# Other places for the running-maximum items of a step in a one-core cross-attention kernel

## The chip, the cores and the metric

The kernel runs on one core of a Trainium2 chip. The metric is the device time of one execution in microseconds (us), median over runs; lower is better. TensorE (PE in the profile) multiplies, VectorE (DVE), ScalarE (ACT) and GpSimd (POOL) work on its results, and SyncE (SP) issues most transfers.

## The reference, cut to what matters

```python
x = layernorm(hidden_states) * ln_gamma + ln_beta        # hidden_states: 2 x 512 x 1024
Q = split_heads(x @ Wq.T)                                # 32 heads of 32
K = split_heads(memory_keys); V = split_heads(memory_keys)   # the context: 2 x 1024 x 1024
scores = einsum('bhsd,bhtd->bhst', Q, K) * 32 ** -0.5    # masked
probs = softmax(scores)
attn = einsum('bhst,bhtd->bhsd', probs, V)
out = residual + merge_heads(attn) @ Wout.T
```

## The kernel before, in words

Sixteen steps (0 to 15) carry the attention; a step is one group of four heads of one batch. Before them the queries are projected, after them the output is projected. A step has eight tiles of 128 context positions. For a tile, TensorE makes four score blocks of 128x512 (one for each head, `score`, L947), in three PSUM banks SX used in turn; ScalarE makes each one's exponential (L615); then the probabilities are multiplied with the values (`values`, L963, eight small matmuls into 32 columns each), one tile later.

Beside this stream runs a second one through two larger PSUM buffers MX, used in turn. Its items belong to other steps and are woven between scores and values:

- `max`: the maximum over keys for a later step. Two score matmuls of 97x512 (`max_item`, L923), then one 128x1024 reduce on VectorE (L737). There are 16 of them for each step, numbered 0 to 15.
- `keys`: eight transposes of the keys of the step two ahead (`keys_item`, L863); ScalarE copies their rounded high part (L541, KTh), VectorE makes the rest (L700, KTl), and only then is the buffer free. SyncE then sends both, and the split queries (L730, L732), to the stacked rows R.
- `bias`: the transposed maxima (L928), copied by ScalarE (L569) and VectorE (L743) and sent to R for the next step's scores.
- `sums`: the row sums of the previous step's probabilities (L953, 24 matmuls); VectorE transposes them (L753).
- `wout`: transposed output weights, in the last two steps alone.

Three lists say where items stand. In a tile, TensorE's order is: scores of heads 0 and 1; the slot's first part (`early`); the previous tile's values; the second part (`with_01`); scores of heads 2 and 3; the third part (`with_23`):

```python
score(n, u, tt, 0); score(n, u, tt, 1)
for item in early: mx_item(*item)
values(n, u, tt - 1)
for item in with_01: mx_item(*item)
score(n, u, tt, 2); score(n, u, tt, 3)
for item in with_23: mx_item(*item)
```

The values of tile 0 are those of the last tile of the step before. Each item waits first, in TensorE's own queue, for the buffer that it takes:

```python
pe.wait_ge(mx_freed, freed - (kind != "bias" or last_kind != ("max", M_ITEMS - 1)))
```

`freed` counts all items before this one, so an item other than the bias goes when all but its immediate predecessor have been released, and the bias when all have. `mx_freed` is raised by VectorE alone, in the order of the items: by the reduce of a `max`, after KTl for `keys`, after BTl for `bias`, after the transpose for `sums`. VectorE walks through the same lists; after a tile's items it adds the reciprocal (tile 2) and the second transpose (tile 3) of the row sums. GpSimd adds up probability tiles 0 to 5 (L486) and normalises (L474).

`FIRST_STEP` places the items of step 0, `STEP` those of steps 1 to 14 (`maxima(a, i)` is item i for the step a ahead). Items for steps past the last are dropped: step 14 has no `keys(2)` and no `maxima(2, ...)`, and step 15 has lists of its own. Steps 1 to 12 are a loop with four steps in its body; 13 to 15 are written out.

Of the kernel before, what the change touches and what calls it, by code (L numbers as in the profile page):

```python
# [66 lines left out]
def keys(a):  # L67
    return [("keys", a, 0)]


def maxima(a, *items):
    return [("max", a, i) for i in items]
# [6 lines left out]
def bias(a):  # L79
    return [("bias", a, 0)]  # L80
# [6 lines left out]
def sums(a):  # L87
    return [("sums", a, 0)]
# [14 lines left out]
    ([], bias(1) + maxima(2, 0), maxima(2, 1, 2, 3)),  # L103
]
STEP = [
    ([], maxima(1, 4), keys(2)),
    ([], sums(-1), maxima(1, 5)),
    ([], maxima(1, 6), maxima(1, 7)),
    (maxima(1, 8), maxima(1, 9), maxima(1, 10)),
    ([], maxima(1, 11), maxima(1, 12)),  # L110
    (maxima(1, 13), maxima(1, 14), maxima(1, 15)),
    ([], bias(1) + maxima(2, 0), maxima(2, 1)),
    ([], maxima(2, 2), maxima(2, 3)),
]


# [1005 lines left out]
```

## Time and profile before

| | |
|---|---|
| median of three runs | 724.67 us (724.27 to 725.08) |
| the profiled execution, its own time | 724.74 us |
| its span, first to last instruction | 722.9 us |
| mean granted TensorE clock | 0.983 |
| TensorE busy with matmuls | 679.7 us, 94% of the span |
| VectorE / ScalarE / GpSimd busy | 460.7 / 339.4 / 392.1 us |
| attention steps 1 to 14 | about 187 to 599 us |

Times in rows are microseconds from the span's start. A row of the timeline is a run of like instructions: start, length, engine, line, output and input, count, and in brackets the idle time ahead of it with what ended it. Matmul ends are modelled, so that neighbouring rows overlap; distances between starts are the safer measure. PEld is the load of weights.

### The profile page before, as it was taken

Reading aid. Unit: us, or ns where it says so; the run is one execution under the profiler, and the core shown is the slowest. Engines: PE = TensorE matmul, PEld = TensorE weight load, DVE = VectorE, ACT = ScalarE, POOL = GpSimd, SP = SyncE. Lnnn points to the kernel's source line nnn. Section 1 sums busy time; section 2 is a strip of 40 time slices with the busy share of each in tenths; the row PEclk is TensorE's granted clock in tenths of the full one; section 3 lists DMA queues with packets and bytes.
Section 4 is the critical chain, followed back from the end, with each engine's and each line's share of the span. In section 5 each row is a group of like instructions: output and inputs, shape, how many; then the busy total and the mean of one; then the engine's idle time right before and its main releaser. Section 6 shows DMA issues by size and latency. Waiting matters only on the chain.

```text
span 722.9 us, 10760 instructions
## 1 busy us (share of the span) xinstructions
PE 679.7 (94%) x3537; PEld 396.9 (55%) x3537; DVE 460.7 (64%) x494; ACT 339.4 (47%) x614; POOL 392.1 (54%) x107
## 2 busy tenths in 40 slices
PE   2789999777999999999999999999999999899998
PEld 2568787633444444444445445454445445478886
DVE  6763333058787787877877868778687676643231
ACT  3741211252566656566666565665666566500000
POOL 1000000054397887967979769797797797910000
PEclk9999999976999999999999999999999999999999
DMA  9611000533335154261442523525325103123231
GB/s 339 189 51 53 30 29 1 135 69 98 75 89 141 51 131 101 64 156 43 123 118 61 143 60 103 133 57 131 85 76 132 60 2 118 58 92 116 84 116 58
DMA packets 40286, 68.10 MB, mean 94 GB/s; under 512 B 5668, under 2 KB 22694, under 8 KB 40238
## 3 DMA queue, kind: packets, MB, share of 16 engines
q1 hardware_dynamic: 39700, 66.85, 33.8%
q10 hardware_dynamic: 548, 0.80, 0.4%
q8 instruction: 17, 0.28, 0.2%
q14 instruction: 21, 0.17, 0.1%
HBM read 25.18 MB, written 4.19 MB: 41 GB/s over the span
## 4 chain that ended last, share of the span: by engine, by line
PE 87%; DVE 5%; ACT 3%; SPq 2%; DMA 2%; issue 2%; POOL 0%; ACTq 0%; DVEq 0%; POOLq 0%
PE MX L923 20%; PE PV L963 18%; PE SX L947 18%; PE MX L1081 12%; PE MX L953 5%; PE SX L886 5%; PE PV L886 4%; PE MX L863 2%; ACT PR L615 1%; PE SX L878 1%; PE MX L933 1%; DMA PR<-in_x 1%; ACT PR L525 1%; PE MX L857 1%; DVE QT L732 1%
## 5 line engine op out<-in xcount | busy, mean ns | idle before, releaser
L737 DVE TENSOR_REDUCE mx<-MX 128x1 f32<-128x1024 f32 x256 | 302.1, 1217 | 107.9 <-PE MX L923 103.3
L615 ACT ACTIVATE PR<-SX 128x512 f32<-128x512 f32 x512 | 269.0, 600 | 173.9 <-PE SX L947 168.4
L486 POOL TENSOR_TENSOR acc<-acc,PR 128x2048 f32<-128x2048 f32 x64 | 293.5, 4587 | 18.0 <-ACT PR L615 11.8
L486 POOL TENSOR_TENSOR acc<-PR 128x2048 f32<-128x2048 f32 x16 | 73.5, 4592 | 224.2 <-ACT PR L615 224.2
L923 PE MATMUL MX<-R 97*128 97x512 f32 x512 | 175.9, 427 | 11.3 <-DVE mx L737 9.2
L947 PE MATMUL SX<-R 99*128 99x512 f32 x512 | 175.4, 420 | 7.5 <-DMA R<-BTl 4.1
L923 PEld LDWEIGHTS MX<-R 97*128 97x128 f32 x512 | 85.6, 190 | 107.9 <-DVE mx L737 89.7
L963 PE MATMUL PV<-PR,C 128*32 128x512 f32 x1024 | 139.0, 615 | 0.1
L947 PEld LDWEIGHTS SX<-R 99*128 99x128 f32 x512 | 94.5, 191 | 70.7 <-ACT PR L615 35.4
L832 DVE TENSOR_TENSOR PR<-PR,MX 128x512 f32<-128x512 f32 x16 | 10.9, 687 | 53.3 <-PE MX L1081 51.9
L1081 PE MATMUL MX<-R 128*128 128x512 f32 x192 | 44.3, 390 | 0.0
L963 PEld LDWEIGHTS PV<-PR,C 128*32 128x32 f32 x1024 | 20.3, 108 | 41.7 <-ACT PR L615 36.8
L1081 PEld LDWEIGHTS MX<-R 128*128 128x128 f32 x192 | 36.0, 188 | 8.3 <-issue 0.8
L1081 PE MATMUL MX<-R,KTh 128*128 128x512 f32 x128 | 40.2, 390 | 0.0
L886 PE MATMUL PV<-R 128*128 128x512 f32 x120 | 31.3, 408 | 0.2 <-DVE R L696 0.2
L700 DVE TENSOR_TENSOR KTl<-MX,KTh 128x1024 fp32r<-128x1024 f32 x15 | 18.4, 1225 | 19.2 <-ACT KTh L541 19.2
L953 PE MATMUL MX<-PR,ones 128*32 128x512 f32 x240 | 28.5, 592 | 0.0
L1081 PEld LDWEIGHTS MX<-R,KTh 128*128 128x128 f32 x128 | 24.0, 188 | 5.8 <-issue 0.8
L474 POOL TENSOR_TENSOR QA<-QA,rsum 128x512 f32 (+1 forms) x16 | 20.7, 1293 | 11.5 <-DVE rsum L759 11.5
L563 ACT ACTIVATE QA<-SX 128x512 f32<-128x512 f32 x8 | 4.8, 598 | 46.7 <-PE SX L886 39.4
L886 PE MATMUL SX<-R,KTh 128*128 128x512 f32 x80 | 25.5, 389 | 0.0
L1081 PE MATMUL MX<-R,KTl 128*128 128x512 f32 x64 | 24.9, 389 | 0.0
(84 smaller groups left out, 478.5 us busy)
## 6 DMA issues: line engine op xcount, KB each, us to landing
R<-KTh SPq DMA_DIRECT2D x60, 256.0 KB, 4.3
PR<-in_x SPq DMA_DIRECT2D x16, 512.0 KB, 4.1
C<-in_ctx SPq DMA_DIRECT2D x16, 512.0 KB, 3.5
R<-KTl SPq DMA_DIRECT2D x60, 128.0 KB, 3.9
R<-QT SPq DMA_DIRECT2D x60, 128.0 KB, 2.5
acc<-in_L_xattn_Wq SPq DMA_DIRECT2D x8, 512.0 KB, 3.5
C<-in_L_xattn_Wout SPq DMA_DIRECT2D x8, 512.0 KB, 3.3
R<-QT SPq DMA_DIRECT2D x60, 64.0 KB, 2.1
```

The lines of the kernel that those rows point to most:

```text
L474: nc.gpsimd.tensor_tensor(at, at, rsum[:, :], ALU.mult).then_inc(attn_done, 1)
L486: nc.gpsimd.tensor_tensor(acc[:, :, :], a, PR[:, tt % RING, :, :], ALU.add).then_inc(pool_used, 1)
L615: nc.scalar.activation(PR[:, tt % RING, h, :], SX[(HPG * tt + h) % BANKS][:, :], ACT.Exp, scale=SCALE).then_inc(exp_done, 1)
L700: nc.vector.tensor_tensor(KTl[:, :], MX[par][:, :], KTh[:, :].bitcast(F32), ALU.subtract).then_inc(kt_lo, 1)
L737: nc.vector.tensor_reduce(mx[:, u % 2, i:i + 1], MX[par][:, :], mybir.AxisListType.X, ALU.max, negate=True).then_inc(mx_freed, 1)
L863: ins = nc.tensor.transpose(MX[par][:, t * P:(t + 1) * P], C[u % RING][:, t, :], ident[:, :])
L886: ins = nc.tensor.matmul(QP[b if bank is None else bank][:, :], w[W_IN[g]][:, k * P:(k + 1) * P], v[b][:, k, :], start=(k == 0 and o == 0) ...
L923: ins = nc.tensor.matmul(MX[par][:, cs], QS[u % RING][0:BIAS, h, st * P:(st + 1) * P], KS[u % RING][0:BIAS, h, cs], start=True, stop=True)
L947: nc.tensor.matmul(SX[at % BANKS][:, :], KS[u % RING][0:ROWS, h, tt * P:(tt + 1) * P], QS[u % RING][0:ROWS, h, :], start=True, stop=True). ...
L953: ins = nc.tensor.matmul(bank[h * HD:(h + 1) * HD, :], ones[:, :], tile(h), start=start, stop=stop, skip_group_check=True)
L963: ins = nc.tensor.matmul(PV[h * HD:(h + 1) * HD, :], C[u % RING][:, tt, h * HD:(h + 1) * HD], PR[:, tt % RING, h, :], start=(tt == 0), sto ...
L1081: ins = nc.tensor.matmul(MX[1 - q][:, cs], a[q][:, g, :], w[half][:, g, :], start=(g == 0 and o == 0), stop=(g == GROUPS - 1 and o == 2))
```

## The change

The 16 maxima of a step keep their order, as do keys, bias and sums between their neighbours in VectorE's list, except that the keys come one maximum later and the sums two. A tile's first item now stands ahead of its values, in `early`, and not behind them. Tiles 0 and 1 have three items instead of two; tiles 3 and 5 have two instead of three. `FIRST_STEP` is as before.

```diff
 STEP = [
-    ([], maxima(1, 4), keys(2)),
-    ([], sums(-1), maxima(1, 5)),
-    ([], maxima(1, 6), maxima(1, 7)),
-    (maxima(1, 8), maxima(1, 9), maxima(1, 10)),
-    ([], maxima(1, 11), maxima(1, 12)),
-    (maxima(1, 13), maxima(1, 14), maxima(1, 15)),
+    (maxima(1, 4), maxima(1, 5), keys(2)),
+    (maxima(1, 6), sums(-1), maxima(1, 7)),
+    (maxima(1, 8), [], maxima(1, 9)),
+    (maxima(1, 10), [], maxima(1, 11)),
+    (maxima(1, 12), [], maxima(1, 13)),
+    (maxima(1, 14), [], maxima(1, 15)),
     ([], bias(1) + maxima(2, 0), maxima(2, 1)),
-    ([], maxima(2, 2), maxima(2, 3)),
+    (maxima(2, 2), [], maxima(2, 3)),
 ]
```

## Rows read from the trace of the kernel before

**Rows 1.** The page: engines' busy time, share of the span, instructions.

```profile
PE 679.7 (94%) x3537; PEld 396.9 (55%) x3537; DVE 460.7 (64%) x494; ACT 339.4 (47%) x614; POOL 392.1 (54%) x107
```

**Rows 2.** The page: the chain that ended last, by engine.

```profile
PE 87%; DVE 5%; ACT 3%; SPq 2%; DMA 2%; issue 2%; POOL 0%; ACTq 0%; DVEq 0%; POOLq 0%
```

**Rows 3.** Timeline of TensorE, tiles 3 and 4 of step 5.

```profile
317.27 0.65 PE L947 MATMUL SX<-R 99*128 99x512 f32 x2
317.81 0.73 PE L923 MATMUL MX<-R 97*128 97x512 f32 x2
318.47 1.06 PE L963 MATMUL PV<-PR,C 128*32 128x512 f32 x8
319.47 0.73 PE L923 MATMUL MX<-R 97*128 97x512 f32 x2
...
320.51 0.63 PE L923 MATMUL MX<-R 97*128 97x512 f32 x2
320.98 0.65 PE L947 MATMUL SX<-R 99*128 99x512 f32 x2
321.61 1.06 PE L963 MATMUL PV<-PR,C 128*32 128x512 f32 x8
...
324.12 0.65 PE L947 MATMUL SX<-R 99*128 99x512 f32 x2
```

**Rows 4.** Timeline: weight loads of two maxima, and VectorE's reduces beside them.

```profile
316.57 0.42 PEld L923 LDWEIGHTS MX<-R 97*128 97x128 f32 x2
...
317.81 0.30 PEld L923 LDWEIGHTS MX<-R 97*128 97x128 f32 x2 [0.20 <-DVE mx L737]
```

**Rows 5.** Timeline of VectorE: the reduces of maxima 6 and 7 in step 5.

```profile
316.53 2.36 DVE L737 TENSOR_REDUCE mx<-MX 128x1 f32<-128x1024 f32 x2 [0.98 <-PE MX L923]
```

**Rows 6.** Timeline: tiles 6 and 7 of step 5, VectorE and TensorE.

```profile
330.75 2.35 DVE L737 TENSOR_REDUCE mx<-MX 128x1 f32<-128x1024 f32 x2 [0.23 <-DVE BTl L743]
...
331.20 0.63 PE L947 MATMUL SX<-R 99*128 99x512 f32 x2
```

**Rows 7.** Timeline: tiles 0 and 1 of step 6, all engines.

```profile
334.45 0.99 PE L947 MATMUL SX<-R 99*128 99x512 f32 x2
...
337.14 1.23 DVE L737 TENSOR_REDUCE mx<-MX 128x1 f32<-128x1024 f32 x1 [1.22 <-PE MX L923]
...
337.41 1.04 PE L863 MATMUL MX<-ident,C 128*128 128x128 f32 x8
...
338.56 1.03 ACT L541 ACTIVATE KTh<-MX 128x1024 fp32r<-128x1024 f32 x1
...
339.62 1.23 DVE L700 TENSOR_TENSOR KTl<-MX,KTh 128x1024 fp32r<-128x1024 f32 x1 [1.26 <-ACT KTh L541]
...
339.73 1.90 PE L953 MATMUL MX<-PR,ones 128*32 128x512 f32 x16
```

**Rows 8.** Timeline: tiles 0 and 1 of step 5, the first of a loop body.

```profile
307.56 0.51 PE L947 MATMUL SX<-R 99*128 99x512 f32 x1 [0.44 <-ACT PR L615]
...
307.90 1.04 PE L863 MATMUL MX<-ident,C 128*128 128x128 f32 x8
...
310.40 1.90 PE L953 MATMUL MX<-PR,ones 128*32 128x512 f32 x16
310.41 1.23 DVE L700 TENSOR_TENSOR KTl<-MX,KTh 128x1024 fp32r<-128x1024 f32 x1 [2.27 <-ACT KTh L541]
```

**Rows 9.** Timeline: the same place in step 9.

```profile
425.45 0.51 PE L947 MATMUL SX<-R 99*128 99x512 f32 x1 [0.16 <-ACT PR L615]
```

**Rows 10.** Timeline: the end of step 0 and the start of step 1.

```profile
184.29 4.62 DVE L737 TENSOR_REDUCE mx<-MX 128x1 f32<-128x1024 f32 x4
...
187.26 0.62 PE L947 MATMUL SX<-R 99*128 99x512 f32 x2
```

**Rows 11.** Timeline of SyncE's queue: last issue of query rows, and bias, in step 6.

```profile
353.08 0.59 SPq L329 DMA_DIRECT2D R<-QT  x1
359.87 0.52 SPq L350 DMA_DIRECT2D R<-BTh  x1
```

## The prediction, made before the changed kernel was run

> **What bounds the kernel now.** I read first the engines' busy time [rows 1]: TensorE is busy for 94% of the span, and no other engine for more than 64%. The chain that ended last says the same [rows 2]: 87% of it is TensorE's own work. So in the attention steps the end is set by the number of TensorE instructions and by the moments in which TensorE's queue waits. The edit adds no work and takes none away. It can only remove waits and make new ones, and the timeline of one step shows where.
>
> The distance from a pair of scores to the next pair is the cost of a tile. Tile 4, with two maxima, runs from 320.98 to 324.12: 3.14 us. Tile 3, with three, runs from 317.27 to 320.98: 3.71 us [rows 3]. A maximum in an ordinary place costs 0.47 us (320.51 to 320.98); the early third one costs 3.71 - 3.14 = 0.57. Why 0.10 more: maximum 8 needs the buffer of maximum 6, whose reduce starts at 316.53. I take 1.23 us for a reduce [rows 5, 7], so it ends at 317.76, and the weights of maximum 8 are loaded at 317.81 with VectorE named as the releaser [rows 4]. From a reduce's end to the load pass 0.05 us.
>
> **The change, part by part.**
>
> Tiles 2 to 5. Before they cost 2 x 3.14 + 2 x 3.71 = 13.70 us and hold ten maxima. Now they hold eight. A new tile is scores, early maximum, values, scores, maximum. The pieces, by the distance to the next start [rows 3]: scores 0.47 or 0.48 (as at 320.51 for a maximum), the maximum ahead of values 0.63 (317.81 to 318.47 is 0.66 with its load exposed, 320.98 to 321.61 is 0.63 for scores ahead of values), values 1.00 (318.47 to 319.47), then a pair behind values and one more 1.04 (319.47 to 320.51): 3.15 us. The same pieces stand in a tile without an early item, only in another order. Is the early maximum free to go? It needs the reduce of the early one a tile back, over two microseconds ahead; VectorE spends 2.4 us on two reduces [rows 5] of a 3.15 us tile, and tiles 2 and 3 add a reciprocal and a transpose, together under a microsecond. I followed VectorE's queue through these tiles and find at most 0.05 us of wait, at maximum 14. So tiles 2 to 5 cost 4 x 3.15 = 12.60, 1.10 less. Two maxima at 0.47 (0.94) have gone to tiles 0 and 1, so the true gain is 0.16 a step. It is the two waits of 0.10 us less the 0.04 that four tiles of 3.15 cost over 3.14.
>
> Tiles 0 and 1, the first new wait. Before, the order was maximum 4, keys | sums, maximum 5. The sums needed only the buffer of maximum 4. Now it is 4, 5, keys | 6, sums, 7: the sums take the buffer of maximum 5, but have to wait for everything but their immediate predecessor 6, and so for the keys' release. That release is slow: transposes on TensorE from 337.41, ScalarE's copy at 338.56, VectorE's subtraction 339.62 to 340.85 [rows 7]. From the keys' start it is 3.44, with the signal 3.49 us. TensorE's cover from the keys' start to the sums is 339.73 - 337.41 = 2.32 us, plus now maximum 6: 2.79. The sums wait for 3.49 - 2.79 = 0.70 us, and behind them in TensorE's queue wait everything: scores, and so ScalarE's exponentials. ScalarE can't start the copy sooner, since it starts 0.1 us after the transposes end; nor can VectorE, which is idle for 1.26 us ahead of its part [rows 7]. Next late would be maximum 6's reduce, behind the subtraction and the query split; it ends near the end of the 2.6 us of sums, before maximum 7 wants it. SyncE's key and query rows start 0.47 us later. The last is issued at 353.08, the maxima that read them start in tile 6, beside the bias whose rows are sent at 359.87 [rows 11], so nothing waits.
>
> The order ahead of the keys is free: maximum 4's reduce, 337.14 to 338.37 before, stays about where it was less a microsecond since its matmuls move ahead of the values, and maximum 5's takes its place and ends near 338.85, when maximum 6 wants to be loaded.
>
> Tile 7, the second new wait. Maximum 2 now stands right behind the first scores, at 331.20 + 0.47 = 331.67. It needs the reduce of maximum 0, which starts only at 330.75 since VectorE makes the bias first [rows 6], and ends at 331.98. The load is then at 332.03, the values 0.66 behind at 332.69, where without a wait they would be at 331.67 + 0.63 = 332.30. It costs 0.39 us. Before, the values stood in between and covered it. The stall at the start of the next step (0.99 us for a pair of scores at 334.45 [rows 7]) does not absorb this: it comes from exponentials that are themselves released by the scores two places back, and so moves along.
>
> Whether a waiting maximum's load could be hidden decides a small part. In an ordinary place the load starts ahead of the matmul (316.57), in a waiting one with it (317.81 for both) [rows 3, 4]; so I charge it. The Trainium skill, TensorE: Matmul & The Clock Gate, section "Architectural detail: the array is 16× 32×32, not 1× 128×128", says that TensorE's queue can pull weight loads ahead of matmuls in flight. By that rule the tile 7 term would be 0.36 and the sum some 0.4 us lower; the trace shows it for loads that wait for nothing.
>
> Steps. Keys and both new waits exist in steps 1 to 13: 13 x (0.70 + 0.39 - 0.16) = 12.1 us. Three corrections. At steps 5 and 9, the starts of a loop body, ScalarE comes late and TensorE already waits for it, at 307.56 and 425.45 [rows 8, 9]. The added maximum fills that wait: the keys stay at 307.90, the release is at 310.41 + 1.23 + 0.05 = 311.69, the sums slip from 310.40 by 1.29, of which 0.94 is the two maxima. That is 0.35 in place of 0.70: -0.7 for both. In step 1 maximum 4 needs the reduce of maximum 2, third of four that start at 184.29 (ending near 187.8) [rows 10], and is loaded about 0.1 to 0.2 late: +0.2. Step 14 has the tiles 2 to 5 alone: -0.16. Sum: 12.1 - 0.7 + 0.2 - 0.2 = 11.4 us.
>
> Bounds. The wait of the sums could be as low as 0.5 (a release that comes a little sooner since ScalarE is less pressed) and as high as 0.9 (a restart of the 32-column matmuls, for which no row stands); the tile 7 wait 0.25 to 0.5; the gain of tiles 2 to 5 up to 0.3, or down to nothing if VectorE's backlog reaches maximum 14. Over 13 steps the ends are about 0.45 and 1.4 a step, some 5 and 18 us; not all at once, so for the range I hold 6 to 15.
>
> **The rivals.**
>
> 1. Forecast: both waits appear. 724.7 + 11.4 = 736.1 us. The profiled execution (724.74) is within 0.1 of the median, so the sum stands against either.
> 2. Only the sums' wait: the tile 7 wait is covered, if maximum 0's reduce came 0.4 us sooner or the matmuls ahead ran later. For it: only 0.39 us and a chain of three engines. Against it: the times at 330.75 and 331.67 leave no cover. 11.4 - 13 x 0.39 = 6.3: 731.0.
> 3. Only the tile 7 wait: the keys' chain gets shorter by 0.7 us. Against it: ScalarE and VectorE already start within 0.1 us. Eleven steps at 0.70 and two at 0.35 are 8.4; 11.4 - 8.4 = 3.0: 727.7.
> 4. The other side, faster: the item buffers are never what TensorE waits for, and only the two released reduces and the filled stalls at loop starts count. The mechanism is that the keys' release reaches TensorE within its cover; it decides from 0.70 us sooner on, and the same must hold in tile 7. 13 x -0.16, another -0.9 for the maxima that fill the stalls at steps 5 and 9 (0.47 each at most), -0.2 for step 14: -3.2, so 721.5. For it: ScalarE and VectorE have free time at both places. Against it: the free time lies behind TensorE's own output, not ahead of it.
> 5. Backlog: VectorE, pushed back 1.6 us at tile 1 by both the split queries and maximum 6, doesn't catch up before maximum 14 and the bias, which waits for maximum 15's reduce; another 0.3 us a step, 740.
> 6. Nothing changes, if each wait removed is one made: within 0.2%, 724.7. It needs the new waits to be a sixth of what I find.
>
> From a maximum to the values pass 0.66 us where to scores it is 0.47 [rows 3]; the change of matmul shape costs that. The values are still entered and left once a tile, and values and sums stay neighbours in tile 1, so the sum has nothing for it.
>
> **How the numbers follow.** Chances: forecast 0.66, only the sums' wait 0.11, only tile 7 0.06, faster 0.05, no change 0.03, backlog 0.09. The predicted time is the forecast's, 736.1. The range from 730.5 to 740.0 takes in rivals 2 and 5 and leaves out 3, 4 and 6 and a little of the forecast's tails, under 2 in 10. A measurement of this kernel can tell about 0.2% (1.4 us) from no change. Faster by more than that 0.05, within it 0.04 (rival 6 and a part of 3), slower 0.91.
>
> **What the profile after would show.** In an ordinary step: a gap of 0.6 to 0.8 us ahead of the first matmuls of L953, released by VectorE's KTl (L700) or its release; in tile 7 a load of L923 weights some 0.05 us behind the end of the first reduce after BTl; tiles 2 to 5 of 3.15 us each with loads of early maxima ahead of their matmuls; the step 30.2 us where it is 29.3. At steps 5 and 9 no wait of L947 over 0.3 us for the exponential, and a slip of about 1.3 for the sums. The prediction is wrong if the sums start without a gap (then the release is not what I take it for), if the values in tile 7 are not held, or if waits of over 0.1 us stand at maxima 10, 12 or 14 (then VectorE's backlog is larger than I worked out).

## The result and the profile after

The changed kernel takes 732.28 us (median of four runs, 731.71 to 733.42) where the kernel before takes 724.47 beside it: a ratio of 1.0109, 95% interval 1.0093 to 1.0125, slower by about 8 us. The prediction said 736.1 with a range of 730.5 to 740.0. The direction and both waits that it named are there; its sum was 11.4 us and the measured difference is 7.8. The profiled execution took 731.71 us with a span of 729.9.

The page of the changed kernel, engines and the chain that ended last:

```profile
PE 677.1 (93%) x3537; PEld 390.7 (54%) x3537; DVE 462.8 (63%) x494; ACT 340.8 (47%) x614; POOL 392.6 (54%) x107
...
PE 75%; DVE 9%; ACT 6%; POOL 3%; issue 3%; SPq 2%; DMA 2%; ACTq 0%; DVEq 0%; POOLq 0%
```

The work is the same as in [rows 1]. The chain [rows 2] was 87% TensorE; now it leaves TensorE for VectorE and ScalarE in every step. The granted clock is 1.00 from 200 to 600 us in both kernels, so the steps don't differ by the clock. The view of waits, from 200 to 610 us, says where (engine, line, releaser: us in total, times, longest):

```profile
PEld SX L947 <- ACT PR L615: 72.1, 155, 0.8
...
PEld MX L953 <- DVEq L702: 18.3, 12, 1.7
...
PEld MX L923 <- DVE mx L737: 8.0, 13, 0.6
...
PE MX L953 <- DVEq L702: 7.4, 12, 0.8
```

The first line looks the largest and costs little: 49 of its 72.1 us are stretches of 0.84 us in which no weights are loaded while the values run, put down to ScalarE. L702 is the release of the keys' buffer: twelve steps in this window, twelve waits. The thirteen of L923 answer to maximum 2 in tile 7.

Since the stream is in order, a step is best read by where its blocks of values start. These are the L963 rows of step 6 in the changed kernel, tiles 0 to 7, and the first of step 7:

```profile
339.94 1.06 PE L963 MATMUL PV<-PR,C 128*32 128x512 f32 x8
...
343.85 1.06 PE L963 MATMUL PV<-PR,C 128*32 128x512 f32 x8
...
350.30 1.06 PE L963 MATMUL PV<-PR,C 128*32 128x512 f32 x8
...
353.37 1.06 PE L963 MATMUL PV<-PR,C 128*32 128x512 f32 x8
...
356.43 1.07 PE L963 MATMUL PV<-PR,C 128*32 128x512 f32 x8
...
359.50 1.06 PE L963 MATMUL PV<-PR,C 128*32 128x512 f32 x8
...
362.17 1.06 PE L963 MATMUL PV<-PR,C 128*32 128x512 f32 x8
...
366.36 1.07 PE L963 MATMUL PV<-PR,C 128*32 128x512 f32 x8
...
369.93 1.06 PE L963 MATMUL PV<-PR,C 128*32 128x512 f32 x8
```

Their distances, as medians over steps 1 to 12 of each trace (worked out from such rows; d0 is from the block in tile 0 to that in tile 1, d7 leads into the next step), for both kernels and the versions tried below, with the medians of the timed runs:

```
                       d0    d1    d2    d3    d4    d5    d6    d7   step   time us
before                3.48  5.25  3.70  3.14  3.71  3.14  3.34  3.57  29.33  724.47
after                 3.91  6.46  3.08  3.08  3.07  2.67  4.19  3.56  30.03  732.28
x1 tile 7 back        3.94  6.44  3.08  3.07  3.08  2.67  3.26  4.03  29.57  727.57
x2 sums not waiting   3.49  5.65  3.71  3.07  3.08  2.67  4.19  3.57  29.43  724.22
x3 both               3.48  5.65  3.71  3.07  3.08  2.67  3.26  4.03  28.95  718.14
x4 two tiles alone    3.47  5.65  3.08  3.70  3.07  3.13  3.35  3.57  29.02  719.84
x7 tile 7 part alone  3.47  5.24  3.71  3.14  3.72  3.14  4.24  3.10  29.74  729.07
x8 none ahead         3.95  6.03  3.13  3.14  3.13  3.14  3.35  4.03  29.90  731.46
x9 bias behind        3.47  5.65  3.70  3.08  3.08  3.11  3.14  3.57  28.79  717.01
```

Before against after: 0.7 us a step, with gains in d2 to d5 that are partly items moved elsewhere, and losses in d0 (0.43, all of it one maximum), d1 (1.21, of which one maximum is about 0.40) and d6 (0.85, of which one maximum is 0.47). From the block in tile 0 of step 1 to that of step 15 the trace grows from 411.45 to 418.46 us. Ahead of that stretch stands the maximum added to step 1, with 0.66. Together this is 7.7 of the 7.8 us.

**The wait of the sums.** TensorE, ScalarE and VectorE in step 6 of the changed kernel:

```profile
341.96 1.04 PE L863 MATMUL MX<-ident,C 128*128 128x128 f32 x8
...
343.12 1.03 ACT L541 ACTIVATE KTh<-MX 128x1024 fp32r<-128x1024 f32 x1
...
344.18 1.23 DVE L700 TENSOR_TENSOR KTl<-MX,KTh 128x1024 fp32r<-128x1024 f32 x1 [1.26 <-ACT KTh L541]
345.51 0.16 PEld L953 LDWEIGHTS MX<-PR,ones 128*32 128x32 f32 x8 [1.51 <-DVEq L702]
345.51 1.92 PE L953 MATMUL MX<-PR,ones 128*32 128x512 f32 x16 [0.60 <-DVEq L702]
```

From the keys' start to the subtraction's end are 3.45 us, as in [rows 7]. The sums start 0.10 us after that and 3.55 after the keys, where they used to start 2.32 after them. Behind the values they would have started at 343.85 + 0.88 = 344.73 (0.88 is their distance in the trace of before); they start 0.78 later.

**The wait of maximum 2** in tile 7, same step:

```profile
364.42 3.49 DVE L737 TENSOR_REDUCE mx<-MX 128x1 f32<-128x1024 f32 x3 [0.23 <-DVE BTl L743]
364.88 0.63 PE L947 MATMUL SX<-R 99*128 99x512 f32 x2
365.70 0.30 PEld L923 LDWEIGHTS MX<-R 97*128 97x128 f32 x2 [0.63 <-DVE mx L737]
365.70 0.73 PE L923 MATMUL MX<-R 97*128 97x512 f32 x2 [0.19 <-DVE mx L737]
```

The reduce of maximum 0 starts at 364.42 and takes 1.23; the load follows at 365.70, where the matmul was due at 364.88 + 0.47 = 365.35. It is the picture that the prediction drew from [rows 6].

**What it did not draw**, tile 3 of the changed kernel:

```profile
355.40 0.64 PE L947 MATMUL SX<-R 99*128 99x512 f32 x2
355.55 0.19 PEld L947 LDWEIGHTS SX<-R 99*128 99x128 f32 x1 [0.18 <-ACT PR L615]
...
355.65 0.42 PEld L923 LDWEIGHTS MX<-R 97*128 97x128 f32 x2
355.88 0.62 PE L923 MATMUL MX<-R 97*128 97x512 f32 x2
```

The second score of the pair waits for ScalarE (0.18), as it did before, but the maximum follows at the ordinary 0.48 and the values start 0.55 behind the maximum (356.43), not 0.63. The new tile takes 3.07 us and not the 3.15 of the prediction.

### The profile page after: what moved, and what is told of

Its sections match the earlier page's. It is cut to its first block, busy times and chain, and to the rows that moved or that the text cites. A ratio compares the mean times of both kernels' runs of the same rounds, so it can differ in the third digit from the quotient of the medians.

```text
span 729.9 us, 10760 instructions
## 1 busy us (share of the span) xinstructions
PE 677.1 (93%) x3537; PEld 390.7 (54%) x3537; DVE 462.8 (63%) x494; ACT 340.8 (47%) x614; POOL 392.6 (54%) x107
## 3 DMA queue, kind: packets, MB, share of 16 engines
HBM read 25.18 MB, written 4.19 MB: 40 GB/s over the span
## 4 chain that ended last, share of the span: by engine, by line
PE 75%; DVE 9%; ACT 6%; POOL 3%; issue 3%; SPq 2%; DMA 2%; ACTq 0%; DVEq 0%; POOLq 0%
PE SX L947 16%; PE PV L963 15%; PE MX L923 14%; PE MX L1081 12%; PE MX L953 6%; PE PV L886 5%; PE SX L886 4%; POOL acc L486 3%; DVE mx L737 3%; DVE KTl L700 2%; ACT KTh L541 2%; ACT PR L615 2%; PE SX L878 1%; DMA PR<-in_x 1%; PE MX L933 1%
## 5 line engine op out<-in xcount | busy, mean ns | idle before, releaser
L737 DVE TENSOR_REDUCE mx<-MX 128x1 f32<-128x1024 f32 x256 | 305.3, 1215 | 112.8 <-PE MX L923 108.1
L947 PE MATMUL SX<-R 99*128 99x512 f32 x512 | 181.1, 432 | 6.7 <-DMA R<-BTl 3.9
L923 PE MATMUL MX<-R 97*128 97x512 f32 x512 | 167.7, 411 | 13.6 <-DVE mx L737 11.4
L947 PEld LDWEIGHTS SX<-R 99*128 99x128 f32 x512 | 88.5, 190 | 119.1 <-ACT PR L615 82.4
L963 PE MATMUL PV<-PR,C 128*32 128x512 f32 x1024 | 138.0, 611 | 0.1
L923 PEld LDWEIGHTS MX<-R 97*128 97x128 f32 x512 | 93.0, 192 | 57.2 <-DVE mx L737 24.0
L963 PEld LDWEIGHTS PV<-PR,C 128*32 128x32 f32 x1024 | 20.2, 108 | 45.3 <-issue 31.3
L953 PE MATMUL MX<-PR,ones 128*32 128x512 f32 x240 | 28.8, 597 | 8.0 <-DVEq L702 8.0
L886 PEld LDWEIGHTS PV<-R 128*128 128x128 f32 x120 | 22.8, 199 | 4.8 <-DVE R L696 0.7
```

The source lines that it names most:

```text
L737: nc.vector.tensor_reduce(mx[:, u % 2, i:i + 1], MX[par][:, :], mybir.AxisListType.X, ALU.max, negate=True).then_inc(mx_freed, 1)
L886: ins = nc.tensor.matmul(QP[b if bank is None else bank][:, :], w[W_IN[g]][:, k * P:(k + 1) * P], v[b][:, k, :], start=(k == 0 and o == 0) ...
L923: ins = nc.tensor.matmul(MX[par][:, cs], QS[u % RING][0:BIAS, h, st * P:(st + 1) * P], KS[u % RING][0:BIAS, h, cs], start=True, stop=True)
L947: nc.tensor.matmul(SX[at % BANKS][:, :], KS[u % RING][0:ROWS, h, tt * P:(tt + 1) * P], QS[u % RING][0:ROWS, h, :], start=True, stop=True). ...
L953: ins = nc.tensor.matmul(bank[h * HD:(h + 1) * HD, :], ones[:, :], tile(h), start=start, stop=stop, skip_group_check=True)
L963: ins = nc.tensor.matmul(PV[h * HD:(h + 1) * HD, :], C[u % RING][:, tt, h * HD:(h + 1) * HD], PR[:, tt % RING, h, :], start=(tt == 0), sto ...
```

## The experiments

The first four ask whether the two waits are what costs, whether they add, and what the places ahead of the values are worth. Each is timed in five rounds beside the kernel before.

**x1: tile 7 as before.**

```diff
-    (maxima(2, 2), [], maxima(2, 3)),
+    ([], maxima(2, 2), maxima(2, 3)),
```

> The changed kernel with one edit: in tile 7 maximum 2 stands behind the values again. Theory (two new waits): its wait for the reduce of maximum 0, about 0.37 us in each of 13 steps, goes, and 0.08 comes back since the values again follow directly on a score that waited for ScalarE. 13 x -0.29 = -3.8: near 728.5 us, tile 6 to 7 from 4.19 to about 3.4 us and tile 7 about 0.5 longer. Rival (the order of these items is of no account, the time sits with VectorE or ScalarE and only moves on to maximum 3 or to the next step): no change, 732.3.

Measured: 727.57 us, 1.0048 of the kernel before (1.0028 to 1.0069), 4.7 less than the changed kernel (across two sets of runs). The step falls by 0.46 where 0.29 was expected. d6 + d7 fall from 7.75 to 7.29, by the whole of the wait, and the 0.08 does not come back: d6 without its maximum is 3.26, less than the 3.34 of before. Part of this belongs to the bias, which experiment x8 separates.

**x2: the sums with the keys as immediate predecessor.** The sums now take the other buffer, and tile 2 has three items.

```diff
-    (maxima(1, 6), sums(-1), maxima(1, 7)),
-    (maxima(1, 8), [], maxima(1, 9)),
+    ([], sums(-1), maxima(1, 6)),
+    (maxima(1, 7), maxima(1, 8), maxima(1, 9)),
```

> The changed kernel with tile 1 as (nothing; sums; maximum 6) and tile 2 as (7, 8, 9): now the keys are the immediate predecessor of the sums, which so don't wait for their release. Theory: the wait of about 0.78 us at L953 goes in each of 13 steps, 0.08 comes back in tile 1; 13 x -0.70 = -9.1: near 723.2 us, less at steps 5 and 9. Rival (VectorE's backlog, since the reduces of 6 to 10 now come close behind the transpose of the sums): waits of 0.3 us or more at maxima 8 and 10 take half of it, 728 us or more.

Measured: 724.22 us, 1.0007 (0.9993 to 1.0022). Its step 6:

```profile
337.37 1.04 PE L863 MATMUL MX<-ident,C 128*128 128x128 f32 x8
...
339.58 1.23 DVE L700 TENSOR_TENSOR KTl<-MX,KTh 128x1024 fp32r<-128x1024 f32 x1 [1.26 <-ACT KTh L541]
339.70 1.90 PE L953 MATMUL MX<-PR,ones 128*32 128x512 f32 x16
```

The keys' chain is as slow as ever, but the sums start 2.33 us after the keys and no longer wait for its end. d1 falls from 6.46 to 5.65, 0.81: that is what the wait costs. The step falls by 0.60, not 0.70: d0 + d1 lose the wait and one maximum (0.42), d2 gains one and pays 0.63 for it. Three maxima between two blocks of values cost 0.57 to 0.63 for the third in every timed version that has them (3.70 or 3.71 against 3.07 or 3.14), since the third comes too soon for the reduce two back. Here that is maximum 10, whose load waits 0.20 us for the reduce of maximum 8 (at 347.51); the rival wanted waits of 0.3 us or more at maxima 8 and 10, and they did not appear.

**x3: both edits.**

> Both edits together: sums without the keys ahead by two, and maximum 2 behind the values in tile 7. If the two waits are separate things their gains add: -3.8 and -9.1, near 719.4 us, under the kernel before by 5 us. Rival: the two share VectorE's or ScalarE's time and the gains don't add; then it is no faster than the better one alone, 723.

Measured: 718.14 us, 0.9916 (0.9898 to 0.9933). The step is 28.95: 1.08 below the changed kernel, and the two singly gave 0.46 and 0.60. The waits are separate and add. This version is faster than the kernel before by 6 us.

**x4: the kernel before with a maximum ahead of the values in tiles 2 and 4 alone.**

```diff
-    ([], maxima(1, 6), maxima(1, 7)),
+    (maxima(1, 6), [], maxima(1, 7)),
...
-    ([], maxima(1, 11), maxima(1, 12)),
+    (maxima(1, 11), [], maxima(1, 12)),
```

> The kernel before with one part of the change alone: in tiles 2 and 4 the first maximum stands ahead of the values, all else as before. Theory that the second score's wait for ScalarE (0.08 us) is covered by a maximum between it and the values, and that the third items in tiles 3 and 5 lose their wait because the reduces start earlier: tiles 2 and 4 at 3.06 us where they were 3.14, tiles 3 and 5 at 3.53 to 3.55 where they were 3.71; -0.5 in 14 steps, near 717.5 us. Rival, the prediction's own reckoning, in which only the 0.10 us waits at maxima 8 and 13 go: -0.2 a step, near 721.7. Second rival: nothing, 724.5.

Measured: 719.84 us, 0.9939 (0.9923 to 0.9955): 4.3 us, between the two expectations (7 and 2.8). The step falls by 0.31. The two distances that now hold two maxima with one ahead of the values, d2 and d4, are 3.08 and 3.07, as expected. What was wrong is the hope for the third items. This load of maximum 11 in step 6 shows the wait in its new place:

```profile
350.00 0.30 PEld L923 LDWEIGHTS MX<-R 97*128 97x128 f32 x2 [0.21 <-DVE mx L737]
```

Of two such waits (maxima 8 and 13 before) one is left, at 11, because the ten maxima after the sums are spread otherwise: d1 takes one more, at 0.40.

The next four take the remaining terms apart.

**x7: the kernel before with the tile 7 edit alone** (the last line of the change's diff).

> The kernel before with the tile 7 part of the change alone: maximum 2 ahead of the values. Theory: it waits for the reduce of maximum 0 as in the changed kernel, 0.46 us in each of 13 steps, and nothing gives it back: +6.0, near 730.1 us. Rival, the prediction's reckoning: 0.39 a step, +5.1, near 729.2. Second rival (what x1 gained came out of a state that only the changed tiles 0 to 5 leave behind): 724 to 725.

Measured: 729.07 us, 1.0058 (1.0042 to 1.0074): 4.3 us. Step 29.74, 0.41 above before. In its step 5:

```profile
331.79 3.49 DVE L737 TENSOR_REDUCE mx<-MX 128x1 f32<-128x1024 f32 x3 [0.23 <-DVE BTl L743]
...
333.06 0.30 PEld L923 LDWEIGHTS MX<-R 97*128 97x128 f32 x2 [0.53 <-DVE mx L737]
...
333.73 1.06 PE L963 MATMUL PV<-PR,C 128*32 128x512 f32 x8
```

The load is 0.04 behind the end of the reduce (331.79 + 1.23) and the values 0.67 behind the load. This is the prediction's term of 0.39 almost to the digit, and the 0.46 that I had put in its place after x1 was too much. The time grows by less than 13 x 0.41 = 5.3, in part because steps 5, 9 and 13 lengthen by only 0.12, 0.34 and 0.29 us in the trace.

**x8: x1, with the first maxima of tiles 2 to 5 behind the values again.**

```diff
-    (maxima(1, 8), [], maxima(1, 9)),
-    (maxima(1, 10), [], maxima(1, 11)),
-    (maxima(1, 12), [], maxima(1, 13)),
-    (maxima(1, 14), [], maxima(1, 15)),
+    ([], maxima(1, 8), maxima(1, 9)),
+    ([], maxima(1, 10), maxima(1, 11)),
+    ([], maxima(1, 12), maxima(1, 13)),
+    ([], maxima(1, 14), maxima(1, 15)),
```

> The kernel of x1 with the first items of tiles 2 to 5 back behind the values: three items at tiles 0 and 1, two elsewhere, but a maximum ahead of the values at tiles 0 and 1 alone. It splits the redistribution from the places. Theory: a tile of 3.07 us becomes one of 3.14 again, four of them in 14 steps: +0.28 x 14 = +3.9 over x1, near 731.5 us, with the wait of the sums unchanged at 0.8. Rival (all of the gain came from having no third item in tiles 3 and 5): the same as x1, 727.6.

Measured: 731.46 us, 1.0099 (1.0085 to 1.0113), 3.9 above x1, as the theory said (across two sets of runs; by the two ratios it is 3.7). d2 to d4 are 3.13 or 3.14. The remaining part of the 0.33 us a step is in d6, 3.35 for 3.26: with maximum 14 ahead of the values VectorE is done with it sooner, takes maximum 15 at once, and the bias finds everything released: it starts 0.99 behind the values in x1 and 1.04 behind them in x8. So the places ahead of the values give 0.06 or 0.07 a tile and 0.09 at the bias.

**x5 and x6: half exponentials.** In the kernel before (x5) and the changed one (x6) every exponential covers 256 of 512 columns; the rest of the probabilities is left as it was. One run each.

```diff
-nc.scalar.activation(PR[:, tt % RING, h, :], SX[...][:, :], ACT.Exp, scale=SCALE)
+nc.scalar.activation(PR[:, tt % RING, h, 0:S // 2], SX[...][:, 0:S // 2], ACT.Exp, scale=SCALE)
```

> Measures the cause of the 0.07 us: the kernel before with exponentials of half the columns (256 of 512; the other half of the probabilities isn't computed, so this is no version to use). Theory (the second score of a pair waits for ScalarE's exponential of the score three back, and directly ahead of the values that shows): tiles with two maxima fall from 3.14 to 3.07, the long pair of scores at the start of a step (0.99 us) to about 0.65, and the wait of L947's weight load for ScalarE goes from nearly every tile. Rival (from scores into the narrow matmuls of the values it simply takes 0.08 us longer than from a maximum): 3.14 stays.

Measured: 712.24 us. Distances d3 and d5, the tiles with two maxima, are 3.05 and 3.06 where they were 3.14. Step 5:

```profile
313.72 0.30 PEld L923 LDWEIGHTS MX<-R 97*128 97x128 f32 x2 [0.35 <-DVE mx L737]
...
316.64 0.43 PEld L947 LDWEIGHTS SX<-R 99*128 99x128 f32 x2
316.87 0.63 PE L947 MATMUL SX<-R 99*128 99x512 f32 x2
...
317.43 0.16 PEld L963 LDWEIGHTS PV<-PR,C 128*32 128x32 f32 x8 [0.37 <-ACT PR L615]
```

The two loads of the pair no longer have a wait between them, and from scores to values it is 0.56 us now, the same as from a maximum, and 0.63 in [rows 3]. From 200 to 600 us the waits of L947's loads for ScalarE fall from 105 (25.8 us) to 18 (7.4 us). The rival is out: it is not the kind of matmul in front of the values. The kernel before says the same at a pair whose second score does not wait: in step 1, from 187.26 to 187.81, it is 0.55 us. The third maximum (313.72) still waits for VectorE, and d2 and d4 stay at 3.70 to 3.72. The long pair of scores at the start of a step shrinks too: d7 falls from 3.57 to 3.15.

> The changed kernel with exponentials of half the columns, the other half not computed. Both theories: tiles 2 to 4 stay at 3.07 us since nothing there waits for ScalarE in front of the values; and since the keys' chain waits for TensorE's transposes and not for ScalarE's exponentials, the wait of the sums stays at 0.7 to 0.85 us, tile 7's at 0.36 to 0.46. Against it, if the sums wait for a ScalarE that is late: 0.4 or less.

Measured: 722.03 us. From its view of waits, 200 to 600 us:

```profile
PEld MX L923 <- DVE mx L737: 19.1, 26, 0.8
...
PEld MX L953 <- DVEq L702: 17.9, 12, 1.5
...
PEld SX L947 <- ACT PR L615: 11.8, 24, 0.8
...
PE MX L953 <- DVEq L702: 7.0, 12, 0.6
```

With ScalarE at half the load the waits of the sums stay (d1 6.43 for 6.46, L953 7.0 for 7.4), as does tile 7 (d6 4.19), and tiles 2 to 4 stay at 3.07. The waits put down to ScalarE go from 70.4 us in the same window to 11.8, but most of that is a new label: the same idle time behind the values now stands as "issue", 61.7 us where it was 21.9. The two together fall by 19 us. The keys' chain is held by its own three links and not by a busy ScalarE.

**x9: a version from the findings.** x3, with maximum 0 ahead of the bias and maximum 2 ahead of the values again:

```diff
-    ([], bias(1) + maxima(2, 0), maxima(2, 1)),
-    ([], maxima(2, 2), maxima(2, 3)),
+    (maxima(2, 0), bias(1), maxima(2, 1)),
+    (maxima(2, 2), [], maxima(2, 3)),
```

> A version built from the findings: sums as in x2; in tile 6 maximum 0 stands ahead of the values and the bias behind it, so that at tile 7 maximum 2, again ahead of the values, waits for the bias's release only and not for a reduce behind it. Theory: no wait at tile 7, and three more maxima than in x3 cover a pair of scores: tiles 5 to 7 at about 9.84 us in place of 9.96 and the step at 28.85 in place of 28.95, so near 716.7 us, 1 us or so under x3. Rival (the bias, now behind the reduce of maximum 0 on VectorE, is released later and maximum 2 waits for that; or the bias rows come late for the next step): 0.3 us or more a step, 721 or more.

Measured: 717.01 us, 0.9887 (0.9871 to 0.9904). The step is 28.79, and tiles 5 to 7 take 3.11 + 3.14 + 3.57 = 9.82 us for the 9.96 of x3. Here the loads of the maxima around the bias (0, 1 and 2) in one step:

```profile
354.93 0.30 PEld L923 LDWEIGHTS MX<-R 97*128 97x128 f32 x2
...
357.13 0.30 PEld L923 LDWEIGHTS MX<-R 97*128 97x128 f32 x2 [0.17 <-DVE mx L737]
...
357.95 0.43 PEld L923 LDWEIGHTS MX<-R 97*128 97x128 f32 x2
```

Maximum 2 (357.95) goes without a wait, from the same place in which it loses 0.4 us in the changed kernel. It is the fastest version run, 1.1% under the kernel before. That it is faster than x3 is shown by the step in the traces; the intervals of the two times overlap.

## Why the prediction was right, and where its size was off

- **Which engine bounds**: right. The work is the same, and what moved was waits in TensorE's queue.
- **The wait of the sums**: right in place and releaser; sized 0.70, it cost 0.81 (d1, x2 against after), inside the bounds of 0.5 to 0.9. Small parts were short: the sums start 3.55 behind the keys and not 3.49 and the cover is 2.77 and not 2.79, which makes 0.78; no run places the last 0.03. One statement on the way was wrong without an effect on the sum: the sums take the keys' buffer, not maximum 5's. The order alternates between two buffers, 4, keys, sums on one and 5, 6 on the other. So the wait is not a quirk of a count that waits for more than it needs; the buffer itself is in use. In x2 the sums take the other buffer.
- **The wait of maximum 2**: right. Sized 0.39; alone (x7) it costs 0.41 a step. In the changed kernel it shows as 0.46 on top of a tile 6 that is 0.09 quicker, since VectorE's side does not move up as much as TensorE does: together 0.37.
- **Tiles 2 to 5, the term that was mis-sized**: "the maximum ahead of values 0.63 ..., 3.15 us" and so a gain of 0.16 a step. I took the 0.63 from scores to values to be the price of entering the values, whatever stands in front, and reckoned that "the same pieces stand in a tile without an early item, only in another order". The row that speaks against it was in my own view of the kernel before: the second score of a pair waits about 0.19 us for ScalarE, here in the pair at 320.98:

```profile
321.13 0.19 PEld L947 LDWEIGHTS SX<-R 99*128 99x128 f32 x1 [0.19 <-ACT PR L615]
```

  Directly ahead of the values this costs 0.07 to 0.08; a maximum in between hides it. x5 shows the cause (0.56 with short exponentials), x8 the size (0.06 to 0.07 a tile). The two waits of 0.10 at maxima 8 and 13 give 0.20, the blocks of values in tiles 2 to 5 some 0.25 (d1 to d4, with 0.47 for each maximum moved), the one in tile 1 0.04 (d0), and there is no backlog: about 0.50 a step outside tiles 6 and 7 where 0.16 was forecast.
- **The sum again, by measured terms**: 0.81 + 0.37 - 0.50 = 0.68 a step, against 0.93. The trace has 30.03 - 29.33 = 0.70. Thirteen steps at 0.25 less are 3.2 us of the 3.6 that the sum was too high; step 14, which has only the gain, is another 0.4.
- **The corrections**: steps 5 and 9 take 30.52 and 30.25 us where they took 30.23 and 29.95, so 0.3 each in place of 0.7. The forecast of -0.7 for both holds (it is -0.8): the added maximum fills TensorE's wait for a late ScalarE. In step 5 the pair of scores ahead of the keys took from 306.72 to 307.90 with 0.44 idle [rows 8]; after, it takes 0.65, and from the step's first scores to the sums are 7.44 us where there were 6.17, a slip of 1.27 for the forecast 1.29. In step 1 the added maximum costs 0.66 us, 0.19 over an ordinary one; 0.2 was forecast.

```profile
310.98 0.82 PE L947 MATMUL SX<-R 99*128 99x512 f32 x2
...
311.63 1.04 PE L863 MATMUL MX<-ident,C 128*128 128x128 f32 x8
```

- **The rivals**: the time came out at the place of rival 2 (only the sums' wait, 731.0), but not by its mechanism; both waits are there. The time came out low because a gain was sized too small, and that it came out just there is chance. It is a case in which the time alone would have named the wrong story. Rival 4, faster, has the direction of x3 but not its size: x3 gains 6.0 us where the rival had 3.2, again for the gain that was sized too small. Its condition, no wait for a buffer at either place, is what x2 and x1 bring about. Rival 5, VectorE's backlog, is in no trace.
- The sentence on weight loads: the waiting load of maximum 2 starts with its matmul in the changed kernel too (365.70 for both), so the charge of 0.03 stands.

## What to carry to other kernels

Where one engine's queue weaves several streams through two buffers, write down for each item which buffer it takes, who releases that, and how long after its start; then every item must stand further from its buffer's last user than that time (here 3.5 us for the keys, 1.9 for a maximum, against pieces of 0.5 and 1.0). A rearrangement should be tried part by part: of this one, two of its moves cost 15 us (13 steps at 0.81 + 0.37) and the rest gained about 7 (14 at 0.50), and the total of 8 slower hid that the other moves, with the two waits avoided, are 0.8% faster than the kernel before (x3), and 1.1% with the bias moved too (x9). And a distance between two instructions in a trace is no constant of theirs until one has looked whether the first of them was itself waiting.

## What was not expected of the hardware

A wait of 0.19 us at a weight load, repeated in nearly every tile and never shown as idle time of TensorE's matmuls, was worth 0.07 us a tile: the matmuls' busy time does not show it, the idle time of PEld does. The switch from the 128-column matmuls to the 32-column ones takes 0.55 or 0.56 us from the start of a pair, whether the pair is of scores or of a maximum, once nothing in it waits; after a pair whose load waited it takes 0.66.
